# Linear attention on one Trainium2 core: the tile of 128 tokens handled as two chunks of 64, in 64-wide tiles of the array

## The reference

```python
qf, kf = elu(rope(q)) + 1, elu(rope(k)) + 1
def step(carry, inp):            # one token after the other
    state = state + k_s[..., :, None] * v_s[..., None, :]
    z = z + k_s
    num = einsum('bhe,bhed->bhd', q_s, state)
    den = einsum('bhe,bhe->bh', q_s, z)[..., None] + EPS
    return (state, z), num / den
out = out_of_all_tokens @ Wo.T
```

## Time and profile before

| what | value |
|---|---|
| median of 3 runs | 1032.81 us (1032.09 to 1033.21) |
| the profiled execution | 1031.37 us, span 1029.6 us |
| TensorE busy (matmuls) | 976.8 us, 95% |
| TensorE weight loads | 791.1 us |
| VectorE | 681.7 us, 66% |
| ScalarE | 332.3 us |
| GpSimd | 249.5 us |

### The profile page before, as it was taken

The page is one execution under the profiler, slowest core; times in us unless marked ns, Lnnn a source line. Parts: engine busy times, 40 slices in busy tenths (PEclk is TensorE's granted clock), DMA queues, the critical chain, the costliest instruction groups (busy, mean ns, idle before and its releaser), DMA issues. The chain is left out here.

```text
span 1029.6 us, 15693 instructions
## 1 busy us (share of the span) xinstructions
PE 976.8 (95%) x5994; PEld 791.1 (77%) x5994; DVE 681.7 (66%) x1494; ACT 332.3 (32%) x604; POOL 249.5 (24%) x320
## 2 busy tenths in 40 slices
PE   5899999999999999999978999998999999999997
PEld 4688888888888888888856788885666667778875
DVE  6766766666766667666565977765676776476556
ACT  4343333433333343334313323221122232422220
POOL 2232312222212323122201010023334554211011
PEclk9999999999999999999998999999999999999999
DMA  9400000000000000000004000002455340000000
GB/s 297 142 1 1 1 1 1 1 1 1 1 1 1 1 1 2 1 1 1 1 21 137 1 1 1 1 1 42 124 115 113 92 84 22 1 16 16 11 21 20
DMA packets 33051, 33.37 MB, mean 32 GB/s; under 512 B 6857, under 2 KB 26834, under 8 KB 32978
## 3 DMA queue, kind: packets, MB, share of 16 engines
q1 hardware_dynamic: 32978, 32.38, 11.9%
HBM read 23.98 MB, written 8.13 MB: 31 GB/s over the span
## 5 line engine op out<-in xcount | busy, mean ns | idle before, releaser
L396 POOL TENSOR_TENSOR rope_sum<-rope_cos,rope_sin 128x512 f32<-128x512 f32 x80 | 115.0, 1437 | 257.0 <-DVE rope_sin L517 257.0
L432 ACT ACTIVATE rope_exp<-rope_sum 128x512 f32<-128x512 f32 x80 | 50.5, 631 | 205.2 <-POOL rope_sum L396 205.1
L786 PE MATMUL proj<-wo_sb,attn_out_t 128*128 128x256 f32 x512 | 113.2, 379 | 0.7 <-issue 0.7
L786 PEld LDWEIGHTS proj<-wo_sb,attn_out_t 128*128 128x128 f32 x512 | 96.1, 190 | 13.4 <-issue 0.9
L735 PE MATMUL num<-v_ones,score_masked 128*128 128x129 f32 x512 | 99.2, 275 | 5.9 <-DVE score_masked L575 5.9
L736 PE MATMUL num<-state,q_t 128*128 128x129 f32 x512 | 99.0, 275 | 0.0
L2052 DVE SCALAR_TENSOR_TENSOR m_acc<-m_expert,gates,m_acc 128x256 f32<-128x256 f32 x128 | 61.9, 484 | 46.3 <-PE m_expert L2101 39.9
L735 PEld LDWEIGHTS num<-v_ones,score_masked 128*128 128x128 f32 x512 | 82.1, 191 | 13.4 <-DVE score_masked L575 8.0
L514 DVE TENSOR_TENSOR rope_cos<-proj,cos_sb 128x512 f32<-128x512 f32 x80 | 55.3, 691 | 52.3 <-PE proj L689 52.3
L689 PE MATMUL proj<-w_hi,a_h_hi 128*128 128x512 f32 x192 | 79.0, 493 | 4.1 <-DVE w_lo L139 2.4
L736 PEld LDWEIGHTS num<-state,q_t 128*128 128x128 f32 x512 | 77.7, 192 | 0.0
(11 more groups left out here) (250 smaller groups left out, 1883.6 us busy)
## 6 DMA issues: line engine op xcount, KB each, us to landing
kv_scratch<-t_kv SPq DMA_DIRECT2D x16, 256.0 KB, 2.4
kv_rows<-kv_scratch SPq DMA_DIRECT2D x32, 128.0 KB, 3.7
a_stage<-in_wqkv SPq DMA_DIRECT2D x6, 512.0 KB, 5.3
wo_sb<-in_wo SPq DMA_DIRECT2D x1, 2048.0 KB, 9.6
a_stage<-in_wgu SPq DMA_DIRECT2D x4, 512.0 KB, 9.7
out<-x_sb SPq DMA_DIRECT2D x16, 128.0 KB, 1.7
u_scratch<-u_rows SPq DMA_DIRECT2D x28, 64.0 KB, 2.9
t_u<-u_scratch SPq DMA_DIRECT2D x14, 128.0 KB, 2.2
```

The costliest lines, as they stand in the source:

```text
L396: pool.tensor_tensor(y[:, parity], t1[:, parity], t2[:, parity], ALU.add).then_inc(s["y_done"], 1)
L786: mm = pe.matmul(proj[:, b, 0:D], o_t[:, i, :], wo[:, i, :], start=(i == 0), stop=(i == H - 1))
```

## The change

A tile of 128 tokens becomes two chunks of 64 (`side` 0 and 1; `HP` = 64).

- Scores: two matmuls, keys of a chunk (64 columns of weights) against that chunk's queries (4 heads x 64), into the upper and the lower half of the partitions. The block of chunk 1's queries against chunk 0's keys is no longer computed. The mask is 64 wide.
- Numerators: in two rounds `j` of two heads; in each, four matmuls of 64 rows x 64 columns of the array (masked scores times values of the chunk), then four of 128 rows x 64 columns (queries times state). Chunk 0 uses the state ahead of the tile, chunk 1 uses `mid`, the state after chunk 0.
- Key sums: one matmul of 64 rows for each chunk and group, eight in all, groups 0 and 1 into `num`, 2 and 3 into `score`. They are now those of the next tile and stand ahead of the output projection of this step, behind `norm_turn`; those of the first tile stand behind its first transpose. VectorE forms `mid` and then the new state (two buffers, in turn) from them: four additions of 128 x 258 instead of one of 128 x 516. Each step's scores wait for these (`sum_used`).
- ScalarE's drains of q and of the output write or read with the chunks apart; their sizes are as before.

```diff
-            causal = sb("causal", [P, P])
+            causal = sb("causal", [P, HP])
-            k_t, q_t = sb("k_t", [P, KVH, P]), sb("q_t", [P, KVH, REP * P])
+            k_t, q_t = sb("k_t", [P, KVH, P]), sb("q_t", [P, KVH, 2, REP, HP])
...
                     def masked(g):
                         dve.wait_ge(s["score_full"], at(c, b, KVH, g + 1))
+                        dve.tensor_tensor(am[:, g % 2, 0:REP * HP].rearrange("p (r t) -> p r t", r=REP),
+                                          score[:, g % 2, 0:REP * HP].rearrange("p (r t) -> p r t", r=REP),
+                                          causal[:].unsqueeze(1).broadcast_to([P, REP, HP]),
                                           ALU.mult).then_inc(s["score_free"], 1)
 
+                    def state_sums(c, b):
+
+                        old, new = states[c % 2][:, b], states[(c + 1) % 2][:, b]
+                        halves = [(slice(2, 4), score), (slice(0, 2), num)]
+                        dve.wait_ge(s["sum_full"], at(c, b, 1, 1))
+                        for gs, bank in halves:
+                            dve.tensor_tensor(mid[:, gs].rearrange("p h w -> p (h w)"), bank[:, 0, 0:2 * VW],
+                                              old[:, gs].rearrange("p h w -> p (h w)"), ALU.add).then_inc(s["mid_done"], 1)
+                        for i, (gs, bank) in enumerate(halves):
+                            dve.wait_ge(s["mid_done"], at(c, b, 2, 1 + i))
+                            t = dve.tensor_tensor(new[:, gs].rearrange("p h w -> p (h w)"), bank[:, 1, 0:2 * VW],
+                                                  mid[:, gs].rearrange("p h w -> p (h w)"), ALU.add)
+                        t.then_inc(s["sum_used"], 1)
...
+                    if (c, b) == (0, 0):
+                        state_sums(0, 0)
                     if nxt:
 
                         split(at(c, b, 1, 2), nb, 2 + 1 + at(c, b, 10, 1))
...
-                    dve.wait_ge(s["num_full"], at(c, b, KVH + 1, KVH + 1))
-                    dve.tensor_tensor(state[:, b].rearrange("p (k h) w -> p k (h w)", k=2),
-                                      num[:, :, 0:2 * VW], state[:, b].rearrange("p (k h) w -> p k (h w)", k=2),
-                                      ALU.add).then_inc(s["num_free"], 1)
                     q_rope(4)
                     f(3)
+                    if not last(c, b):
+                        state_sums(c + b, 1 - b)
...
                     def scores(g):
                         pe.wait_ge(s["turn_free"], 2 + 1 + turn_item(c, b, 1 + g))
                         pe.wait_ge(s["score_free"], at(c, b, KVH, g + 1))
-                        pe.matmul(score[:, g % 2, :], k_t[:, g, :], q_t[:, g, :], start=True, stop=True
-                                  ).then_inc(s["score_full"], 1)
+                        pe.wait_ge(s["sum_used"], at(c, b, 1, 1))
+                        for side in range(2):
+                            rows = slice(side * HP, (side + 1) * HP)
+                            mm = pe.matmul(score[rows, g % 2, 0:REP * HP], k_t[:, g, rows],
+                                           q_t[:, g, side].rearrange("p r t -> p (r t)"), start=True, stop=True)
+                        mm.then_inc(s["score_full"], 1)
 
                     def numerators(g):
                         pe.wait_ge(s["score_free"], 2 + at(c, b, KVH, g + 1))
...
+                        for j in range(2):
+                            places = [(side, q, num[q * HP:(q + 1) * HP, side, j * VW:(j + 1) * VW], 2 * j + q)
+                                      for side in range(2) for q in range(2)]
+                            for side, q, dst, r in places:
+                                rows = slice(side * HP, (side + 1) * HP)
+                                pe.matmul(dst, am[rows, g % 2, r * HP:(r + 1) * HP], v[rows, b, g, :], start=True, stop=False)
+                            for side, q, dst, r in places:
+                                mm = pe.matmul(dst, q_t[:, g, side, r, :], mid[:, g, :] if side else states[c % 2][:, b, g, :],
+                                               start=False, stop=True)
                         mm.then_inc(s["num_full"], 1)
 
+                    def sums(c, b):
+
+                        pe.wait_ge(s["num_free"], num_item(c, b, 0) + 1)
+                        pe.wait_ge(s["score_free"], 2 + at(c, b, KVH, 0))
+                        for g in range(KVH):
+                            bank = score if g >= 2 else num
+                            for side in range(2):
+                                rows = slice(side * HP, (side + 1) * HP)
+                                mm = pe.matmul(bank[:, side, (g % 2) * VW:(g % 2 + 1) * VW],
+                                               feat[rows, b, 0, g * P:(g + 1) * P], v[rows, b, g, :], start=True, stop=True)
+                        mm.then_inc(s["sum_full"], 1)
...
                     turn4(0, feat[:, b, 0, :])
+                    if (c, b) == (0, 0):
+                        sums(0, 0)
                     q_turn(0)
...
-                    pe.wait_ge(s["num_free"], at(c, b, KVH + 1, KVH + 1))
-                    for g in range(KVH):
-                        mm = pe.matmul(num[:, g // 2, (g % 2) * VW:(g % 2 + 1) * VW], feat[:, b, 0, g * P:(g + 1) * P],
-                                       v[:, b, g, :], start=True, stop=True)
-                    mm.then_inc(s["num_full"], 1)
                     out_turn(3)
                     p(5)
                     if norm_on:
                         norm_turn(turn_item(c, b, 9), b, bank(9), at(c, b, 1, 3))
+                    if not last(c, b):
+                        sums(c + b, 1 - b)
```

More of the change, by code:

```diff
@@ L300, in attention_phase @@
             state = sb("state", [P, 2, KVH, VW])
+            other = wmod[:].rearrange("p k n -> p (k n)")[:, 0:2 * KVH * VW].rearrange("p (b g w) -> p b g w", b=2, w=VW)
+            states = [state[:], other]
+            mid = self.g_xn[:].rearrange("p i d -> p (i d)")[:, 0:KVH * VW].rearrange("p (g w) -> p g w", w=VW)
             den, rden = sb("den", [P, REP]), sb("rden", [P, REP])
@@ L381, in _ @@
                 pool.wait_ge(s["mask_one"], 1)
-                pool.affine_select(out=causal[:], in_=causal[:], compare_op=ALU.is_ge, fill=0.0, base=0,
-                                   pattern=[[1, P]], channel_multiplier=-1).then_inc(s["causal_made"], 1)
+                for side in range(2):
+                    rows = causal[side * HP:(side + 1) * HP, :]
+                    pool.affine_select(out=rows, in_=rows, compare_op=ALU.is_ge, fill=0.0, base=0,
+                                       pattern=[[1, HP]], channel_multiplier=-1).then_inc(s["causal_made"], 1)
+                    pool.wait_ge(s["causal_made"], side + 1)
                 def rstd_of(n, b):
@@ L730, in numerators @@
+                        mm.then_inc(s["score_full"], 1)
                     def numerators(g):
                         pe.wait_ge(s["score_free"], 2 + at(c, b, KVH, g + 1))
-                        pe.wait_ge(s["num_free"], at(c, b, KVH + 1, g + 1))
-                        for r in range(REP):
-                            dst = num[:, r // 2, (r % 2) * VW:(r % 2 + 1) * VW]
-                            pe.matmul(dst, am[:, g % 2, r * P:(r + 1) * P], v[:, b, g, :], start=True, stop=False)
-                            mm = pe.matmul(dst, q_t[:, g, r * P:(r + 1) * P], state[:, b, g, :], start=False, stop=True)
@@ L737, in numerators @@
-                        mm.then_inc(s["num_full"], 1)
+                        pe.wait_ge(s["num_free"], num_item(c, b, g) + 1)
+                        for j in range(2):
[7 more added lines that the diff above has]
+                                               start=False, stop=True)
@@ L739, in out_turn @@
                     def out_turn(g):
-                        pe.wait_ge(s["num_free"], 1 + at(c, b, KVH + 1, g + 1))
+                        pe.wait_ge(s["num_free"], 2 + num_item(c, b, g))
                         turn4(5 + g, on[:, g % 2, :])
```

20 lines of the change are left out of this document (11 added, 9 removed).

## The result

The changed kernel takes 1059.2 us (median of 4 runs, 1054.95 to 1068.59) against 1033.0 (4 runs, 1032.09 to 1034.43): a ratio of 1.0265, 95% interval 1.0189 to 1.034. It is slower by about 26 us. Medians and ranges in this text are of all runs; ratios leave out those that lie more than 1.5% above the fastest of their kernel. The forecast was 1053, with a range of 1040 to 1066. The profiled execution of the changed kernel took 1062.27 us, span 1060.4.

A forecast was written before the change was run, and what follows sets the result against it. TensorE's stream was taken to bound the step. Steady steps +17.7, first step +4.5, last step -2.1 sum to +20.1 us on 1031.37 profiled, 1051.5 there, hence a median of 1053 us; range 1040 to 1066.

The forecast's parts named there:

- The step's term: Steady attention step on TensorE: 4.37 us of shape changes less 3.19 of streaming, +1.18 us a step, +17.7 over fifteen.
- Streaming: Scores, numerators and key sums on TensorE in a steady step: 8.26 us instead of 11.45, 3.19 less.
- The gap of 0.09 and the load of 0.05 into a 64-wide tile: TensorE entering a 64-wide shape: drain gap plus unhidden first weight load, 0.14 us, 19 times a step.
- the 0.19 for each of the exits: TensorE returning to the full array: 0.09 gap plus 0.10 load for 128-wide weights, 9 times a step.
- Rival 1: Numerators: changes between 64x64 and 128x64 cost nothing, removing 12 a step, 27 us, so 1026 us; chance 0.10.
- Rival 2: 64-row tiles do not overlap in pairs: 1066 us for the sums alone, 1094 with the 64x64 tiles; chance 0.08.
- Rival 3: VectorE's state additions arrive late and hold each step's scores: up to 25 us, 1078 us; chance 0.04.
- the 3.94 us of slack: VectorE's idle time at the end of the output projection, taken to hide the 1.7 us of state additions there.
- Rival 4: Gains and shape changes cancel, nothing measurable; needs 0.11 us a change instead of 0.16 on the mean; chance 0.02.
- The first step: Key sums wait for rden, then additions and the split delay p(0): +4.5 us, between +3 and +6.
- The last step: Attention step without projections, TensorE waiting for VectorE: shorter masks, exposed scores and no sums give -2.1 us.
- Behind the last output projection: Unedited later phases, including the scan: no term in the forecast, difference 0.

The follow-up runs named there:

- e2: Kernel before with only the scores made in two column halves over all 512 columns, eight shape changes a step; step 32.78 us, 1057.2 us, ratio 1.0222.
- e3: Changed kernel with each group's numerators reordered, both 64x64 rounds first, then both 128x64 rounds; step 31.13 us, 1039.1 us, 1.0024 of before.
- e5: e3 with scores of groups 2 and 3 moved ahead of output transposes, right behind the numerators; step 30.44 us, 1029.6 us, 0.9923 of before.
- e1: Changed kernel run again, unedited; step 32.37 us, 1060.8 us, 1.0257 of before.
- e4: Changed kernel with two unused 512-column matmuls put into each of two TensorE waits in the last step; last step 29.3 us, 1058.2 us, 1.0229 of before.
- e6: Changed kernel, first step only: key sums behind the query transposes, VectorE's split of h ahead of the state additions; first output projection 70.5 us, 1059.2 us.
- e11: e5 with 120 already met waits added at the start of TensorE's program; 1026.1 us, 0.993 of before.
- e12: e5 run again, unchanged; step 30.44 us, 1026.2 us, 0.9929 of before.
- e8: Kernel before with only the scores of groups 2 and 3 swapped ahead of output transposes; step 31.55 us, 1033.1 us (one run).
- e9: Kernel before with 2600 already met waits added on SyncE to lengthen its program; 1032.8 us, 0.9969 of before.

## Why the forecast held

**The shape of the answer.** Slower, by shape changes that outweigh what streams at once: e2 shows the cost without any gain (+1.25 a step), e3 and e5 take it away with the same matmuls (-1.24 and -0.69). The mechanism was the one named.

**The step's term.** Forecast +1.18, measured +0.84. Streaming was right: 0.24 and 0.455 for the rounds, 0.45 for the scores, and the sums as many passes deep as said. The gap of 0.09 and the load of 0.05 into a 64-wide tile were right too. What was sized wrong is the exit to transposes: their load is recorded at 0.14 us, and the first pass after a change takes 328 ns where most take 272, so 0.05 is exposed and not the 0.10 that I took for every 128-wide tile. A step has five such exits: -0.25. The term that was mis-sized is therefore the 0.19 for each of the exits: for those to transposes it is 0.14. The remaining -0.09 lies in hundredths: 28 changes measure 0.84 + 3.19 = 4.03 us, 0.144 each, against 0.156 in the forecast. Over fourteen steps the term was 4.7 us too high. The passes of the transposes in one step (ns, shortest, median, longest):

```profile
L743 PE MATMUL turn<-ident,feat x30: 272/273/328, 302.1 to 336.0; 128*128 128x128 f32 x30
```

**Rival 1** (the inner changes are free) is wrong: 0.38 and 0.60 in the timeline are both one full change over the streaming, and e3 gives 0.155 back for each change removed. The Trainium skill, TensorEngine Tiling (Array Packing), Key Properties, has it that a change of mode drains TensorE and a change of tile doesn't; the trace agrees, with 0.49 us for the same eight passes when the scores that follow share their shape and 0.60 when another shape follows.

**Rival 2** (64-row tiles are serial) is wrong: sixteen passes in four tiles take 0.60 us with the change in e3; serially they would be 16 x 0.111 = 1.78. The sums, 16 passes in two row halves, take 1.09 (326.38 to 327.47).

**Rival 3** (the additions hold the next scores) is wrong. VectorE in the step of after:

```profile
329.43 0.42 DVE L598 TENSOR_TENSOR g_xn<-score,state 128x258 f32<-128x258 f32 x1
329.76 0.42 DVE L598 TENSOR_TENSOR g_xn<-num,state 128x258 f32<-128x258 f32 x1
330.10 0.42 DVE L602 TENSOR_TENSOR a_wmod<-score,g_xn 128x258 f32<-128x258 f32 x1
330.43 0.42 DVE L602 TENSOR_TENSOR a_wmod<-num,g_xn 128x258 f32<-128x258 f32 x1
334.69 0.42 DVE L684 TENSOR_TENSOR a_dx<-proj,gate_b 128x256 f32<-128x256 f32 x1 [3.84 <-PE proj L832]
```

They cost 4 x 0.42 recorded, as forecast, but start 0.33 apart; they end at 330.85, the scores start 5.6 us later (336.42), and 3.84 of the 3.94 us of slack is still there.

**Rival 4** (gains and changes cancel) needed 0.11 a change: 0.144 was measured. (e3's whole is level with before, but for another reason: its 20 changes leave the step 0.40 shorter, and the rest of the kernel took that back.)

**The first step.** The timeline of after, for the earlier trace rows:

```profile
41.01 0.06 DVE L577 MEMSET rden<- 128x4 f32 x1
...
41.13 1.23 PE L782 MATMUL num<-v_ones,feat 64*128 64x129 f32 x8 [8.14 <-DVE rden L577]
...
43.37 0.43 DVE L598 TENSOR_TENSOR g_xn<-score,state 128x258 f32<-128x258 f32 x1 [2.29 <-PE score L782]
...
44.71 0.28 DVE L512 CAST a_h_hi<-a_h 128x256 fp32r<-128x256 f32 x1
...
46.09 0.72 PE L715 MATMUL proj<-w_hi,a_h_hi 128*128 128x512 f32 x2
```

From rden to p(0) it is 5.08 us, before 0.89: +4.2, forecast +4.5, and each link is there: sums at half clock (2.0 us, to 43.15), four additions, the split, p(0). The other 1.9 us are that rden itself is late (41.01 against 39.15). Nothing ahead of it on TensorE or VectorE was edited; 24.7 to 28.1 us ran at half clock in this execution. The profiles of after, e1, e3, e4, e6, e11 and e12 have a stretch like it, and rden at 40.8 us or later; the other seven have none, and rden at 38.8 to 39.9. e12, which is e5 again, has it (24.0) where e5 had not: it moves between executions of one program. All seven that have it are kernels with the chunks (of ten), none of the four without has it; whether the change makes it more frequent is open. What the forecast counted, from rden to p(0), was right to 0.3 us.

**The last step.** The forecast's -2.1 is -2.5 in e4 at the full clock. In after's own execution half clock turned it into +2.8, in e1's into +0.4. This is not special to the chunks: e8 and e9, with the matmuls of the kernel before, have 3.4 us of half clock in their last step and take 33.1 and 33.2 us for it, while the 31.8 of before, with which all is compared, comes from a profile without any. The forecast had reckoned only with VectorE setting this step and not with what a TensorE that waits for it gets: its passes at 0.64 instead of 0.38 us for eight.

**Behind the last output projection.** Forecast 0; +9.3 in after's profile, +4.3 in e1's. This is the largest error, and it covered the step's: without it, and with the last step at the full clock, the sum would have been 6.9 + 11.8 - 2.5 = 16.2 instead of the forecast's 20.1. That the total came as near as it did is in part luck: errors of opposite sign. That this stretch is longer by as much as half clock and late stores account for is shown to 1.5 us. That instruction packets lie beside every late store is shown over 98 stores. That they cause the delay, and that TensorE's longer program causes the packets to fall there, is argued (q8 58 against 48 in all, though 24 in both behind the last output projection, at other places) and stays open: a program whose fetches miss the stores around 210, 229 and 266 us was not had. e9 doesn't bear on it, since its packets fell elsewhere. Why the granted clock falls more often in these kernels is open as well; one link was seen in after, where `kv_rows` came late and TensorE waited 1.82 us right ahead of a half-clock stretch that starts at 799.5:

```profile
798.86 0.29 DVE L1560 TENSOR_TENSOR u_rows<-kv_rows,z_ps 128x128 f32<-128x128 f32 x1 [2.62 <-DMA kv_rows<-kv_scratch]
799.20 0.56 PE L1773 MATMUL g_ps<-u_rows,kv_rows 16*128 16x128 f32 x8 [1.82 <-DVE u_rows L1560]
799.68 1.22 PE L1740 MATMUL kv_ps<-w_lo,t_h_hi 128*128 128x512 f32 x2
```

The same two places, open as to their cause, are where the gain of e3 and e5 went: e5's steps are 1.09 us shorter than before, 14 x 1.09 = 15.3 us between the first and the last, and the medians of its program lie 4 to 8 us below before's. Its profile has +2.8 up to the first output projection, -2.4 in the last step and +16.2 behind it; e12's has +4.6, -1.4 and +3.1.

## What to carry to other kernels

Splitting a matmul into array tiles pays by what streams at once and costs by every change between shapes, also between two tiled ones: count both per group before writing it, here 3.19 us gained against 28 changes of 0.14. Put all matmuls of one shape next to each other, across groups and across outputs; the same matmuls went from 0.84 us a step slower to 1.09 faster by order. And when a stretch is bound by another engine, or the program grows, look at what the change does to the clock and the transfers of phases that it doesn't touch.

## What was not expected of the hardware

- The price of a change depends on the load that follows: 0.05 us over the gap of 0.09 ahead of transposes with 128 columns (loads of 0.14 us), but 0.11 ahead of the output projection, whose 32 passes take 7.02 us (327.47 to 334.49) instead of 6.91.
- A store of 256 KB and its read-back, 2.03 to 2.09 us apart in 58 cases without an instruction packet between them, were 2.14 to 4.27 apart in 40 cases with one.
- One program (e5 and e12) differs by 13 us in a phase of 500, mostly by how long the granted clock was 0.50: 41 us in all behind the last output projection against 10.
- In a step where TensorE waits for VectorE, two idle gaps filled with matmuls of no use kept the clock at 1.00 and made the step 2.9 us shorter than e1's; eleven of twelve profiles without them have half clock there.
